# Second graph pass of a graph network kernel: one ring wait per four gathers instead of one per gather

## The reference, cut to what matters

```python
def _L1_gnn_ref(x, edge_index, W, a_src, a_dst, gamma, beta):
    hh = (x @ W).reshape(n, H, D)                       # 8 heads of 32
    s_src = jnp.einsum('nhd,hd->nh', hh, a_src)
    s_dst = jnp.einsum('nhd,hd->nh', hh, a_dst)
    scores = jax.nn.leaky_relu(s_src[src] + s_dst[dst], negative_slope=0.2)
    m = jax.ops.segment_max(scores, dst, num_segments=n)
    e = jnp.exp(scores - m[dst])
    denom = jax.ops.segment_sum(e, dst, num_segments=n)
    alpha = e / denom[dst]
    msgs = hh[src] * alpha[:, :, None]
    out = jax.ops.segment_sum(msgs, dst, num_segments=n).reshape(n, H * D)
```

## Time and profile before

| | before |
|---|---|
| median of 3 runs | 5405.28 us (5404.92 to 5430.75) |
| the profiled execution's own time | 5400.45 us |
| its span | 5398.4 us |
| TensorE clock granted, mean of the span | 0.844 |
| L942, the 880 gathers of this pass | 878.1 us busy, 998 ns each |
| L427, the 880 gathers of the first graph's pass | 859.0 us busy |
| L978, PE's sums of this pass, two instructions a step | 727.3 us busy |

### The profile page before, as it was taken

The page is one execution under the profiler, slowest core; times in us unless marked ns, Lnnn a source line. Parts: engine busy times, 40 slices in busy tenths (PEclk is TensorE's granted clock), DMA queues, the critical chain, the costliest instruction groups (busy, mean ns, idle before and its releaser), DMA issues. The chain is left out here.

```text
span 5398.4 us, 69620 instructions
## 1 busy us (share of the span) xinstructions
PE 3959.7 (73%) x16281; PEld 2855.2 (53%) x16282; DVE 3059.0 (57%) x7623; ACT 1862.2 (34%) x5073; POOL 2462.0 (46%) x2442
## 2 busy tenths in 40 slices
PE   6867777777776659967854667666667338999999
PEld 4545555555554448856732444444444226777776
DVE  3278878778877766662063666666667773111111
ACT  1333433333333313211223444444444322333332
POOL 2256656556656450001166666666663422333332
PEclk8989988889989879987986776777777559999999
DMA  2555545455555332311173333333331451111111
GB/s 79 187 145 156 155 143 150 141 148 152 148 147 146 90 123 78 95 57 38 47 255 89 95 94 95 94 96 94 94 95 52 128 193 21 32 31 31 31 31 27
DMA packets 316127, 553.65 MB, mean 103 GB/s; under 512 B 63430, under 2 KB 213782, under 8 KB 315856
## 3 DMA queue, kind: packets, MB, share of 16 engines
q0 software_dynamic: 137120, 388.63, 26.5%
q1 hardware_dynamic: 178736, 161.98, 9.6%
HBM read 459.75 MB, written 90.62 MB: 102 GB/s over the span
## 5 line engine op out<-in xcount | busy, mean ns | idle before, releaser
L427 POOL DMA_INDIRECT attend_ring<-kv_rows,all_step_src x880 | 859.0, 976 | 630.0 <-PE attend_ps_agg L468 366.3
L942 POOL DMA_INDIRECT edge_ring<-head_rows,all_step_src x880 | 878.1, 998 | 455.6 <-issue 212.6
L978 PE MATMUL edge_ps_agg<-edge_msg,edge_sel 128*128 128x264 f32 x1760 | 727.3, 535 | 221.6 <-issue 65.4
L468 PE MATMUL attend_ps_agg<-attend_msg,attend_sel 128*128 128x264 f32 x1760 | 604.1, 445 | 188.1 <-DVE graph_qa L785 128.6
L978 PEld LDWEIGHTS edge_ps_agg<-edge_msg,edge_sel 128*128 128x128 f32 x1760 | 410.1, 259 | 373.6 <-issue 209.8
L2813 DVE TENSOR_TENSOR moe_gl<-moe_ps_h,moe_act 128x341 f32<-128x341 f32 x210 | 107.8, 514 | 776.8 <-PE moe_ps_h L2731 776.8
L452 PE MATMUL attend_ps_q<-graph_qa,attend_sel_t 128*128 x1760 | 525.8, 428 | 25.2 <-issue 25.2
L1283 DVE TENSOR_TENSOR graph_acc<-graph_acc,edge_ps_agg 128x264 f32 x880 | 369.6, 420 | 296.5 <-PE edge_ps_agg L978 195.4
L785 DVE SCALAR_TENSOR_TENSOR graph_qa<-graph_qa,all_step_same,attend_ps_agg 128x264 f32 x880 | 421.5, 479 | 176.0 <-remote 126.7
L468 PEld LDWEIGHTS attend_ps_agg<-attend_msg,attend_sel 128*128 128x128 f32 x1760 | 329.8, 209 | 352.5 <-issue 150.6
L2731 PE MATMUL moe_ps_h<-experts_w,moe_xt 128*128 x1680 | 501.8, 451 | 0.6 <-ACT moe_xt L2762 0.6
(11 more groups left out here) (424 smaller groups left out, 6470.4 us busy)
## 6 DMA issues: line engine op xcount, KB each, us to landing
attend_ring<-kv_rows,all_step_src POOLq DMA_INDIRECT x880
edge_ring<-head_rows,all_step_src POOLq DMA_INDIRECT x880
kv_rows<-qkv_kv SPq DMA_DIRECT2D x25, 512.0 KB, 2.9
experts_w<-in_w_t SPq DMA_DIRECT2D x16, 682.0 KB
attend_mask<-run_starts SPq DMA_DIRECT2D x440, 8.1 KB
edge_mask<-run_starts SPq DMA_DIRECT2D x440, 8.1 KB
head_rows<-hds_hh SPq DMA_DIRECT2D x25, 264.0 KB
qkv_x<-in_x SPq DMA_DIRECT2D x25, 256.0 KB, 3.2
```

The lines of the kernel that those rows point to most:

```text
L427: nc.gpsimd.indirect_dma_start(ring[:, step % RING1, :], None, g.kv_rows, bass.IndirectOffsetOnAxis(g.step_src[:, step:step + 1], 0)).then ...
L468: nc.tensor.matmul(ps_agg[i % SUM_BANKS][:, 0:AGG], sel[:, q % 2, u % QU, :], msg[:, q % 2, u % QU, :], start=True, stop=True).then_inc(s_ ...
L942: nc.gpsimd.indirect_dma_start(ring[:, n % slots, u, :], None, g.head_rows, bass.IndirectOffsetOnAxis(g.step_src[:, step:step + 1], 0)).th ...
L978: nc.tensor.matmul(ps_agg[i % BANKS][:, 0:AGG], sel[:, q % 2, u % QU, :], msg[:, q % 2, u % QU, :], start=True, stop=True).then_inc(s_agg, 1)
```

## The change

One condition and one bound in POOL's program:

```diff
                 for u in range(CH):
                     step = n * CH + u
-                    if n >= slots:
-                        pool.wait_ge(s_agg, step - slots * CH + 1)
+                    if n >= slots and u % QU == 0:
+                        pool.wait_ge(s_agg, step - slots * CH + QU)
                     nc.gpsimd.indirect_dma_start(ring[:, n % slots, u, :], None, g.head_rows,
```

## The result

The changed kernel is slower: 5473.26 us (median of 4 runs, 5468.32 to 5478.27) against 5410.62 (median of 4) for the kernel before; the ratio is 1.010, with a 95% interval of 1.0082 to 1.0118. That is 63 us more where 18 us less were forecast, and above the range's upper end of 5455.

The account below looks back on a forecast made before the run. The prediction took a chain of hand-overs to bound the kernel, with POOL working nearly all of each turn. Its terms, 0 + 0 - 18 us off the median of 5405.28, gave 5387, with an 8-in-10 range of 5335 to 5455.

Parts of the forecast that it names:

- What bounds the kernel: Mid-pass: a chain of hand-overs, 23.8 us a turn; POOL works nearly all of it and really waits 3.05 us.
- The later the longer the run: While gathers follow each other, PE's results reach other engines later with longer runs: 20 us under 48, 2.9 in short ones.
- 612 waits go, 0 us: Three quarters of the 816 ring waits on POOL's gathers vanish; 0 to 6 us on POOL, taken as 0.
- Late rows, 0: Gathers starting up to 3.9 us later delay only L1183, which has 18 to 24 us in hand; cost 0.
- The last gather, 0: At the pass's end the last gather moves by 3.9 us into 18 us of slack; cost 0.
- The first wait, 0: At the start the first ring wait moves from round 0 to round 3 of chunk 0; cost 0.
- the walk through one turn: POOL's stops in a mid-pass turn: 2.7 us against 3.05, turn 23.5, 18 us less over 51 turns; chance 0.36.
- The slower rival: POOL, credited in fours, stops 1.0 us over the gap at every quarter: turn 24.8, 48 us more, 5454; chance 0.21.
- decision point of 3.6 us: The slower rival decides from 3.6 us of POOL stops a turn on, against 2.7 in the walk.
- The faster rival: Runs of four let PE's results through nearly on time: 84 us less at most, half gives 5363; chance 0.33.
- The rule of the Trainium skill: Engines' and DMA's sides of SBUF cannot slow each other, so the gathers' timing is nothing to PE and the term is 0.
- The signs named in the prediction: Profile after: POOL idle near 400 us (under 350 faster, over 430 slower), gathers busy near 878, L1203's waits near 85.

Follow-up runs that it names:

- rest_pairs_t: The kernel before with a 128 x 512 memset on POOL ahead of every second gather from chunk 4 on, timed on another chip; ratio 0.9992.
- w8: The kernel before with one wait per eight gathers, for the latest of their rounds, instead of one per gather; ratio 1.0154.
- each_plus3: The kernel before, still one wait per gather, but each asking for three rounds more; ratio 1.0017.
- q3_coarse: The kernel before with only the third quarter's gathers grouped behind one wait for round 11, the other twelve waiting one by one; ratio 1.012.
- after_again: The changed kernel timed again, on the chip of a later group of runs; ratio 1.0079 to the kernel before.
- q3_fine: The changed kernel with the third quarter's gathers waiting one by one again; ratio 1.0156 to the kernel before.
- start_paced: The kernel before with the three single waits at the heads of chunks 1 to 3 replaced by one wait a quarter; ratio 0.9995.

## Why the prediction was wrong

*What bounds the kernel* was read rightly. The rows are early by a turn, the turn is shorter without gathers (17.3 us, at a higher clock), PE's results come late while gathers are issued, and the ring's wait sets where runs end. "The later the longer the run" is not borne out: 3.1 us with runs of two (rest_pairs_t), 2.3 with runs of eight and sixteen (w8). *612 waits go, 0 us* held: the gap between two gathers is 0.30 as before. *Late rows, 0* held: 16 us are left, and each_plus3 costs 0.17%. *The last gather, 0* held. *The first wait, 0* did not quite: from the first gather to the first that waits for the ring it is 106.4 us before, 106.5 in q3_coarse, whose first wait is the same, and 109.0 to 111.5 in the four kernels that first wait for round 3 (after, after_again, each_plus3, q3_fine), 3 to 5 us more.

**The step that failed is the walk through one turn**, the term "when POOL runs and stops": 2.7 us of stops a turn, measured 4.33.

| stop before | walk | after, us a turn |
|---|---|---|
| first quarter (round 3) | 1.4 | 62 / 51 = 1.2 |
| second (round 7) | 0 | 18 / 51 = 0.4 |
| third (round 11) | 1.1 | 104 / 51 = 2.0 |
| fourth (round 15) | 0.2 | 33 / 51 = 0.6 |

The first came out; the other three are too small by 1.7 us together. Where the walk lost them is seen in its own terms, the times between DVE's adds L1283 of rounds 3, 7, 11 and 15, in us, averaged over 50 turns:

| from round to round | without gathers | walk | before | after | after_again |
|---|---|---|---|---|---|
| 15 to 3 | 6.5 | 6.5 | 7.4 | 7.0 | 7.1 |
| 3 to 7 | 3.4 | 3.4 | 5.3 | 4.6 | 4.7 |
| 7 to 11 | 3.9 | 8.1 | 6.5 | 8.1 | 8.2 |
| 11 to 15 | 3.2 | 5.2 | 4.8 | 5.3 | 5.0 |
| turn | 17.1 | 23.2 | 23.9 | 25.0 | 25.0 |

(In the walk, 8.1 is the time from 9.9, where round 7 was due, to 18.0.) The second half came out: 4.2 us of lateness for `row` and `ends` and 2.0 ahead of round 15 are what the trace has on average. That is partly luck, as they were read from one turn, and single turns differ widely (the step from 7 to 11 is over 9 us in 30 of the 50 turns after, and between 4 and 6.5 us in most of the others). **What failed is the first half, rounds 0 to 7, which the walk took at the pace without gathers: 9.9 us, measured 11.6** (12.6 before, 11.8 in after_again). It did so although by its own account POOL issues two quarters of gathers in that time, and although the stretch of the earlier trace rows had the clock at 0.90 and the pass has 0.73. The "microsecond or so" by which round 7 is late was used to say that POOL does not stop, and then left out of the time at which round 11 is due. With it round 11 comes 19.7 us after round 15 and not 18.0; these 1.7 us are POOL's extra stops, half of them before gather 8. The walk was not held against the kernel before, where its pace for rounds 0 to 7 would have shown as 2.7 us too short. How the 1.7 us divide between the clock and results that come late is not shown.

**The slower rival** is what happened, in its mechanism: POOL gets its credit in fours, and where PE is one round short it stands for the rest of the quarter. Its decision point of 3.6 us of stops a turn was crossed (4.33). Its form was off: no stop at every quarter of 1.0, but one of 3.0 before the third quarter in two turns of three. Its turn of 24.8 was nearly the measured 24.95; its 48 us are 56 in the pass. I held against it that PE runs free while POOL stops and so pays the stop back. It does not, since POOL works 20.8 of 24 us: every microsecond in which it stands must be made up by a longer turn, whatever PE gains in it.

**The faster rival** needed runs of four; the change left 56 of them and made 72 of eight, against 21 of eight and 21 longer ones before. **The rule of the Trainium skill**, SBUF — State Buffer, section on who interferes with whom, that the engines' side and the DMA's side of SBUF can't slow each other, is not borne out by the runs as a statement on the whole way from PE to the waiting engines: L1203 starts 1.2 us after L992 without gathers and 3.9 with them. Nor do they show that SBUF is where it is lost.

The signs named in the prediction: the idle time after the first ring wait came to 466 us, over the 430 that spoke for the slower case; the gathers' busy time, 868, was near 878; L1203's long waits went from 85 to 102 us by the row named there (88 to 123 by all over 1 us); DVE did not wait in L1183.

Open: what holds PE's counts back while POOL issues gathers (it lies ahead of the count's going up, in PE's work itself or between it and the count, and the rows don't tell which; a matmul's end is modelled), how much of the turn is the clock's, why the third quarter one by one (q3_fine) is no faster than the change, and why groups of eight lose less than twice what groups of four do.

## What to carry to other kernels

A wait that lets an engine run ahead also meters it; before waits are merged into coarser ones, ask how much idle time that engine has in the loop. Here POOL had 3 of 24 us, a group of two cost nothing that could be measured, a group of four 1%, although no transfer was ever late. And when a schedule is walked, do not take a pace from a stretch in which the engine in question is silent and the clock is another, carry every lateness into what follows, and walk the kernel before the same way first: a walk that misses the known turn by more than the effect can't forecast it.

## What the runs showed of the hardware

- PE's counts went up late while POOL issued gathers: DVE's L1203 started 20.0 us after the end of L992 under a run of 48, 7.0 us under one of eight, and 3.9 us on average in the kernel before. Without gathers it was 1.2 us. The trace has the count's rise at most 0.03 us ahead of DVE's start, so the time is lost before it.
- These waits did not have to last to the end of a run: the 20.0 us ended at 2857.0 in the middle of the run of 48, which went on to 2885.4, and after the change 24 of 32 long waits ended in mid-run. In start_paced one lasted 10 us beyond a run of 24, with only four gathers in them.
- A memset of 0.54 us on POOL before every second gather took 23.3 us for L1203's waits in one execution where 95 had been, at the same turn; a second execution of the same kernel on another chip had 73.
- The clock granted in mid-pass was 0.74 with the gathers and 0.90 without them.
- The start of one gather after another took 1.26 us in an unbroken run, with a wait in it or without.
